# x1 read half a group earlier in a graph network kernel, its parts turned at the slot's head and normalised by VectorE

## The chip, the cores and the metric

One core of a Trainium2 chip. The metric is the device time of the program in microseconds (us), as the median of several executions. "Group", "part" and "half" below are the kernel's own units of work.

## The reference, cut to what matters

A graph of 12,500 nodes with 128 features each and 212,500 edges, sorted by destination, goes through two layers. The first is a relational layer (16 relation types, weights composed from 8 bases), the second takes the mean over the neighbours. Each is followed by a residual add and a layer norm without gain or bias.

```python
# layer 1: relational, W = sum over the bases
W = jnp.einsum('rb,bio->rio', w_comp, weight)
msg = jnp.einsum('ni,rio->rno', x, W)[etypes, src]
x1 = _layernorm(x + segment_sum(msg, dst) + h_bias)
# layer 2: mean of the neighbours
deg = jnp.maximum(segment_sum(ones, dst), 1.0)
agg = segment_sum(x1[src], dst)
out = _layernorm(x1 + x1 @ W_self + b_self + agg / deg[:, None] @ W_neigh)
```

## The kernel before

Edges are cut into chunks of 128 and groups of 8 chunks: 208 groups. GpSimd (POOL) gathers the source rows of a chunk with one indirect DMA, 128 rows at a time, into slots in SBUF, and TensorE (PE) sums them into short windows of destination nodes with a one-hot matrix as the moving operand. All order is written out by hand, as loops over g (the group) on each engine, with semaphores between them.

The two layers overlap. Since the edges are sorted by destination, x1 (the first layer's result) is finished front to back, in parts of 256 nodes (PART); part k is complete when all groups below done_at(k) = (17(k + 1) + 7) // 4 have been added, about every 4.25 groups, with 49 parts in all. The first PLAIN = 20 groups gather rows of x only (512 bytes, L1642, "narrow"). From group 20 on POOL gathers "wide" rows (1 KB, L1646) from a table in DRAM with x in the left half and x1 in the right half, where the part has been laid, and zeros where it has not. The table exists twice: in the upper copy the right half stays zero. Before the first wide group VectorE (DVE) marks the edges (mark_early): each half group h of 4 chunks reads x1 from the first front(h) parts, and an edge with a source beyond them goes to the upper copy. So half of the second layer's sum is made while the first layer still runs. The edges that were sent to the upper copy ("late" edges) are packed into full columns of 128 later on, and are gathered again in a second sweep (L1657 for two groups that were held back, L1673 for the rest) with x1 rows. How many columns are needed is fixed when the program is built, from front(h) and an even spread of sources; a flag checks the real data against it.

front(h) comes from READABLE, a distance in half groups: readable(h) = 4 (max(h - READABLE, 2) // 2 - 1) and front(h) = min(FRONT, readable(h) // 17), with FRONT = 44. With READABLE = 4 part k is read from half 2 done_at(k) + 4 on, the first half of group done_at(k) + 2. POOL waits, ahead of the first gather of each half, on the semaphores laid1 of the parts that are new in it (loop over `part`, in the GpSimd block), and on nothing else of theirs. Its slots hold four wide groups, so that for group g it also waits until the slot's last user has been read: `rows_read` for group g - 4, or, for g = 20 and 21, the sums (`z_done`) of the narrow groups 17 and 19.

How a part comes to be, at slot g = done_at(k):

- PE sums group g - 1 (sum_half, L2253, and for the x1 half early_half, L2265), ACT copies the sums out (L1722), PE multiplies them by the 8 bases (project, L2293), DVE adds them to acc (add_sums, L1904).
- PE transposes the part (turn_part, L2221), in program order behind sum_half(g, 0), the first half group's eight matmuls of g itself.
- DVE adds the transposed part to x (L1766), takes statistics (L1772, L1777), ScalarE (ACT) the root (L1690), DVE the reciprocal (L1784) and the shift (L1786), and ACT normalises in two activations, one for each tile of 128 nodes (normalise_quad, L1696).
- SyncE (SP) stores it into the table (L1533, laid1) and into x1_rows (L1535), and the degrees after them (L1526).

The order on DVE at slot g is: add_sums of a finished run, part_done, the pair additions (L1891), the one-hots of group g + 2 (scale, L1859 and L1865). PE's order is sum_half(g, 0), turn_part, early_half(g, 0), sum_half(g, 1), early_half(g, 1), project. Every fourth group PE also makes the coefficients of the next four groups (scale_by_relation, L2240).

Of the kernel before, what the change touches and what calls it, by code (L numbers as in the profile page):

```python
# [40 lines left out]
PART = TPP * P  # L41
PLAIN = 20
READABLE = 4
RUN = 5
# [13 lines left out]
def gnn_kernel(nc, x_in, src, dst, etype, weight, w_comp, h_bias, w_neigh, w_self, b_self, x1_rows, out):  # L58
# [48 lines left out]
    def front(h):  # L107
        return 0 if h < 2 * PLAIN else min(FRONT, readable(h) // 17)

    assert per_group % 2 == 0 and all((readable(h) * 3856) >> 16 == readable(h) // 17 for h in range(2 * groups))  # L110
    assert all(2 * done_at(front(h) - 1) + READABLE <= h < 2 * done_at(front(h)) + READABLE
               for h in range(2 * PLAIN, 2 * groups) if front(h) < FRONT)
    early_share = 16.0 / 17.0 / n_nodes

# [62 lines left out]
    with ctx:  # L177
# [340 lines left out]
        with nc.Block(no_gpsimd_drain=True) as block:  # L518
# [75 lines left out]
            def _(dve):  # L594
# [75 lines left out]
                dve.wait_ge(s_dl, 13)  # L670
                dve.wait_ge(s_held, 9)
                nc.vector.tensor_tensor(thr[:, 0:etiles], thr[:, 0:etiles], lates8[:, :], ALU.add).then_inc(s_held, 1)
                dve.wait_ge(s_held, 10)
                nc.vector.tensor_scalar(expected[:, :], thr[:, 0:etiles], -early_share * P, P * 16.0 / 17.0, ALU.mult,
# [38 lines left out]
                nc.vector.tensor_tensor(loop_n[:, :], loop_n[:, :], not_held[:, :], ALU.mult).then_inc(s_held, 1)  # L713
                dve.wait_ge(s_held, 11)
                nc.vector.tensor_tensor(lates[:, :], lates[:, :], loop_n[:, :], ALU.subtract).then_inc(s_order, 1)
# [486 lines left out]
        with nc.If(in_order):  # L1202
# [260 lines left out]
            with nc.Block(no_gpsimd_drain=True) as block:  # L1463
# [215 lines left out]
                def _(act):  # L1679
# [33 lines left out]
                    for g in range(groups + 8):  # L1713
                        if g * table_step < full_rows:
                            lay_zeros(g * table_step, min((g + 1) * table_step, full_rows))
                        if g in out_at:
                            roots_of(n1, out_at[g])
                            normalise_quad(n1, out_at[g])
                        if g < groups:
                            act.wait_ge(w1.z_done, g + 1)  # L1720
                            after(act, w1.y_done, run_of[g])
                            nc.scalar.copy(zsb[:, kept_at(g)].rearrange("p (h w) b n -> p h (w b n)", h=2),  # L1722
                                           zduos[g % 2]).then_inc(w1.z_copied, 1)
                        if g in loops_at:
                            q, m = quads[loops_at[g]]
                            act.wait_ge(s_loops, loops_at[g] + 1)
                            nc.scalar.copy(loops_b[:, q * P:(q + m) * P], tps[1][:, 0:m, :]).then_inc(s_loopc, 1)
                        if g in cleared_at:
                            clear_part(cleared_at[g])
# [29 lines left out]
                def _(dve):  # L1759
# [20 lines left out]
                    def quad_factors(n, k):  # L1780
# [6 lines left out]
                                                       op0=ALU.mult, op1=ALU.mult).then_inc(n.factors, 1)  # L1787

                    def part_done(k):
                        if k >= 2:  # L1790
# [5 lines left out]
                        quad_stats(n1, k)  # L1796
                        quad_factors(n1, k)

# [414 lines left out]
                def _(pe):  # L2213
# [85 lines left out]
                    for g in range(groups):  # L2299
                        coefficients_due = g % HALF == 2 and g // HALF + 1 < 2 * bodies  # L2300
                        if coefficients_due and g not in out_at:
                            scale_by_relation(g // HALF + 1)
                        sum_half(g, 0)
                        if g in out_at:
                            turn_part(out_at[g])
                            if coefficients_due:
                                scale_by_relation(g // HALF + 1)
                        early_half(g, 0)
                        sum_half(g, 1)
# [389 lines left out]
```

## Time and profile before

| | us |
|---|---|
| median of 3 executions | 3188.19 (3185.18 to 3188.43) |
| the profiled execution, its own time | 3178.99 |
| its span, first to last instruction | 3177.5 |
| PE busy | 2260.3 (71%) |
| DVE busy | 1554.4 (49%) |
| ACT busy | 316.0 (10%) |
| POOL busy | 2381.3 (75%) |
| mean granted TensorE clock | 0.681 of full speed |

The first layer's sweep, with the early half of the second, takes the span up to about 2102 us, the second sweep the rest. Busy time tells little here, as no engine is near 100%. What to read are the chain that ended last, the idle time of POOL with what ended it, and the order in time around one part. "Issue" is time in which an engine waited for nothing that the profile shows. The granted clock goes back and forth between full (2.4 GHz) and half (1.2 GHz) in stretches of 7 to 34 us, and the length of a matmul shows which of the two holds.

### The profile page before, as it was taken

To read this page: it belongs to the slowest core of one execution; us is meant where nothing else is said; L and a number is where in the kernel's file an instruction comes from. 1 tells how busy PE (TensorE), PEld (TensorE's weight loads), DVE (VectorE), ACT (ScalarE), POOL (GpSimd) and SP (SyncE) were. 2 spreads that over 40 slices of the span, in tenths; PEclk is the share of its full clock that TensorE was granted. 3 is DMA by queue.
4 is the path that set the end of the run, shared out by engine and by line. 5 is a ranking of instruction groups with operands and counts; after the bars stand their busy time and mean duration, and the time that the engine had idled before them with its cause. 6 is when DMAs were issued, how large, how long until landed. Compare 5 with 4: busy or idle time off the path is not lost.

```text
span 3177.5 us, 39386 instructions
## 1 busy us (share of the span) xinstructions
PE 2260.3 (71%) x13106; PEld 2164.2 (68%) x13106; DVE 1554.4 (49%) x4520; ACT 316.0 (10%) x619; POOL 2381.3 (75%) x2518
## 2 busy tenths in 40 slices
PE   2678888888878888898888888874555555555454
PEld 1568878888878888898887887864444444454444
DVE  6463333433343333333333333336677776877445
ACT  2111111111111111111111111100000000000012
POOL 7767777777777777777777777777777777777775
PEclk8887776776777777767777667665556555556567
DMA  4944444444444444444444444332222222222333
GB/s 115 312 132 122 121 122 118 121 123 121 123 120 121 119 122 122 122 122 123 122 115 123 123 122 120 111 97 53 63 63 63 73 63 63 73 63 73 89 82 87
DMA packets 257255, 345.05 MB, mean 109 GB/s; under 512 B 46912, under 2 KB 189861, under 8 KB 257046
## 3 DMA queue, kind: packets, MB, share of 16 engines
q0 software_dynamic: 104208, 262.76, 29.8%
q1 hardware_dynamic: 127398, 66.86, 7.1%
q10 hardware_dynamic: 25440, 12.85, 1.4%
q8 instruction: 106, 1.74, 0.2%
q14 instruction: 103, 0.84, 0.1%
HBM read 310.75 MB, written 44.38 MB: 112 GB/s over the span
## 4 chain that ended last, share of the span: by engine, by line
POOL 67%; issue 23%; PE 4%; DVE 1%; DMA 1%; ACTq 1%; ACT 1%; DVEq 0%; SPq 0%; POOLq 0%
POOL rows L1646 42%; POOL rows L1673 25%; PE zps L2253 1%; PE tps L2293 1%; ACTq L1683 1%; DMA rows<-x_x_rows,src_t 1%; POOL rows L1657 0%; DMA x_x_rows<-xout 0%; DVE acc L1904 0%; PE yps L2265 0%; ACT acc L1722 0%; PE tps L2240 0%; DMA erep<-in_edge_type_dram 0%; ACT xout L1696 0%; DVE xout L1766 0%
## 5 line engine op out<-in xcount | busy, mean ns | idle before, releaser
L1646 POOL DMA_INDIRECT rows<-x_x_rows,src_t x1501 | 1424.2, 949 | 469.5 <-issue 453.6
L2253 PE MATMUL zps<-acc,rows 128*128 128x168 f32 x3322 | 758.7, 388 | 285.2 <-DMA rows<-x_x_rows,src_t 280.5
L2253 PEld LDWEIGHTS zps<-acc,rows 128*128 128x128 f32 x3322 | 651.3, 246 | 307.6 <-DMA rows<-x_x_rows,src_t 197.0
L1673 POOL DMA_INDIRECT rows<-x_rows,picked_mem x685 | 647.9, 946 | 208.8 <-issue 208.8
L1904 DVE TENSOR_TENSOR acc<-acc,tps 128x21 f32 x831 | 146.7, 177 | 934.6 <-PE tps L2293 813.9
L2378 PE MATMUL zps<-acc,rows 128*128 128x128 f32 x1370 | 312.4, 400 | 403.2 <-DMA rows<-x_rows,picked_mem 389.4
L2378 PEld LDWEIGHTS zps<-acc,rows 128*128 128x128 f32 x1370 | 269.2, 292 | 438.2 <-DMA rows<-x_rows,picked_mem 270.5
L2293 PE MATMUL tps<-acc,picked_mem 128*128 128x168 f32 (+2 forms) x2288 | 488.5, 388 | 31.6 <-ACT acc L1722 22.6
L2265 PEld LDWEIGHTS yps<-oh,rows 128*128 128x128 f32 x3002 | 508.4, 248 | 0.0
L2293 PEld LDWEIGHTS tps<-acc,picked_mem 128*128 128x128 f32 x2288 | 454.0, 272 | 43.9 <-ACT acc L1722 24.7
L2265 PE MATMUL yps<-oh,rows 128*128 128x21 f32 x3002 | 478.5, 300 | 0.0
L1865 DVE TENSOR_TENSOR acc<-oh,tps 128x1344 f32<-128x1344 f32 x208 | 323.2, 1554 | 30.0 <-PE tps L2240 1.8
L1722 ACT COPY acc<-zps 128x672 f32<-128x672 f32 x208 | 149.0, 716 | 1410.2 <-PE zps L2253 1391.8
L1891 DVE TENSOR_TENSOR acc<-acc,yps 128x42 f32 (+1 forms) x831 | 163.3, 196 | 178.3 <-DVE acc L1891 45.2
L2104 DVE TENSOR_TENSOR acc<-place_b,tps 128x1024 bf16<-128x1024 bf16 x190 | 229.9, 1210 | 0.0
L2018 DVE TENSOR_TENSOR acc<-acc,zps 128x128 f32 (+1 forms) x442 | 118.1, 267 | 218.8 <-PE zps L2378 136.5
L1673 POOL DMA_INDIRECT rows<-x_rows,src_t x144 | 136.0, 944 | 43.9 <-issue 43.9
L2371 PE MATMUL zps<-oh,rows 128*128 128x21 f32 x320 | 74.6, 383 | 84.4 <-DMA rows<-x_rows,src_t 83.3
L1642 POOL DMA_INDIRECT rows<-in_x_dram,src_t x112 | 107.7, 961 | 34.2 <-issue 34.2
L2371 PEld LDWEIGHTS zps<-oh,rows 128*128 128x128 f32 x320 | 71.0, 328 | 88.5 <-DMA rows<-x_rows,src_t 52.1
L1993 DVE TENSOR_TENSOR acc<-picked_mem,tps 128x1024 f32<-128x1024 f32 (+2 forms) x92 | 104.8, 1140 | 0.0
L1690 ACT ACTIVATE std<-mv,epst 128x2 f32<-128x2 f32 (+1 forms) x74 | 21.9, 296 | 698.3 <-DVE mv L1777 698.3
(294 smaller groups left out, 1493.6 us busy)
## 6 DMA issues: line engine op xcount, KB each, us to landing
rows<-x_x_rows,src_t POOLq DMA_INDIRECT x1501, 2.8
erep<-in_edge_type_dram SPq DMA_DIRECT2D x207, 64.0 KB
x_x_rows<-zrow ACTq DMA_DIRECT2D x20, 576.0 KB, 3.7
x_x_rows<-in_x_dram SPq DMA_DIRECT2D x20, 576.0 KB
rows<-x_rows,picked_mem POOLq DMA_INDIRECT x685, 2.5
x_rows<-xout SPq DMA_DIRECT2D x49, 128.0 KB
xin<-in_x_dram SPq DMA_DIRECT2D x48, 128.0 KB
out_dram<-xout SPq DMA_DIRECT2D x24, 256.0 KB, 2.5
```

The lines of the kernel that those rows point to most:

```text
L1646: gather = pool.indirect_dma_start(out=wide_rows[:, g % WIDE_SLOTS, c, :], out_offset=None, in_=table, in_offset=bass.IndirectOffsetOnAxis ...
L1673: pool.indirect_dma_start(out=rows[:, j % SLOTS, c, :], out_offset=None, in_=x1_rows[0:n_nodes, :], in_offset=bass.IndirectOffsetOnAxis(ap ...
L1722: nc.scalar.copy(zsb[:, kept_at(g)].rearrange("p (h w) b n -> p h (w b n)", h=2), zduos[g % 2]).then_inc(w1.z_copied, 1)
L1865: nc.vector.tensor_tensor(a[:, g % 4], oh1[:, g % 6].unsqueeze(2).to_broadcast([P, CPG, n_bases, SPAN]), wcp[:, m % 2, g % HALF, :].rearra ...
L1891: add = nc.vector.tensor_tensor(target, target, windows_of(g)[:, first:2, c, :], ALU.add)
L1904: add = nc.vector.tensor_tensor(target, target, bank_of(run_of[g])[:, y0:y0 + SPAN], ALU.add)
L2104: nc.vector.tensor_tensor(to_lane[:, t % UNROLL], place_b[:, 0, at].unsqueeze(2).to_broadcast([P, CPG, P]), lanes_p.unsqueeze(1).to_broadc ...
L2253: last = nc.tensor.matmul(zwins[g % 2][:, c // HALF, c % HALF // 2], slot_rows(g, c), a[:, g % 4, c], start=(c % 2 == 0), stop=(c % 2 == 1 ...
L2265: last = nc.tensor.matmul(windows_of(g)[:, 0, c // 2], wide_rows[:, g % WIDE_SLOTS, c, d:2 * d], oh1[:, g % 6, c], start=(c % 2 == 0), sto ...
L2293: last = nc.tensor.matmul(bank_of(r)[:, y0:y0 + duos * SPAN].rearrange("p (w n) -> p w n", n=SPAN), wb[:, b, :], kept[:, 0:duos, b, :], st ...
L2371: last = nc.tensor.matmul(sums_of(j, c // 2, SPAN), rows[:, j % SLOTS, c, :], oh1[:, j % 4, c], start=(c % 2 == 0), stop=(c % 2 == 1))
L2378: last = nc.tensor.matmul(sums_of(j, c0, P), rows[:, j % SLOTS, c, :], oh2[:, j % 4, c, :], start=(c == c0), stop=(c == c0 + n - 1))
```

## The change

- READABLE goes from 4 to 3. Since readable(h) is rounded down to whole groups, this changes odd halves alone: part k is read from half 2 done_at(k) + 3 on, the second half of group done_at(k) + 1.
- The first four wide groups (SETTLING = 8 halves) read the first three parts alone (FIRST_PARTS); the threshold in `thr` gets the same bound by two more DVE instructions in the preamble.
- PE turns a part ahead of sum_half(g, 0).
- The part's normalisation moves from ACT to DVE: the shift and ACT's two activations go, and DVE does (x - mean) * rstd in place with two tensor_scalar instructions.

```diff
-READABLE = 4
+READABLE = 3
+FIRST_PARTS = 3
+SETTLING = 8
...
     def front(h):
-        return 0 if h < 2 * PLAIN else min(FRONT, readable(h) // 17)
+        if h < 2 * PLAIN:
+            return 0
+        return min(FIRST_PARTS if h < 2 * PLAIN + SETTLING else FRONT, readable(h) // 17)
...
-                dve.wait_ge(s_held, 9)
+                nc.vector.tensor_scalar(half_v[:, :], half_i[:, :], float(2 * PLAIN + SETTLING), FAR, ALU.is_ge,
+                                        ALU.mult).then_inc(s_held, 1)
+                dve.wait_ge(s_held, 10)
+                nc.vector.scalar_tensor_tensor(out=thr[:, :], in0=half_v[:, :], scalar=float(FIRST_PARTS * PART), in1=thr[:, :],
+                                               op0=ALU.add, op1=ALU.min).then_inc(s_held, 1)
+                dve.wait_ge(s_held, 11)
...
                         if g in out_at:
                             roots_of(n1, out_at[g])
-                            normalise_quad(n1, out_at[g])
...
+                    def normalise_part(k):
+                        dve.wait_ge(n1.std, k + 1)
+                        m = part_tiles(k)
+                        nc.vector.reciprocal(rstd[:, 0:m], std[:, 0:m]).then_inc(n1.rstd, 1)
+                        dve.wait_ge(n1.rstd, k + 1)
+                        for j in range(m):
+                            normed = x_out_of(n1, k)[:, j, :]
+                            last = nc.vector.tensor_scalar(normed, normed, mv[:, j, 0:1], rstd[:, j:j + 1], ALU.subtract, ALU.mult)
+                        last.then_inc(n1.norm, 1)
...
                         quad_stats(n1, k)
-                        quad_factors(n1, k)
+                        normalise_part(k)
...
-                        sum_half(g, 0)
                         if g in out_at:
                             turn_part(out_at[g])
                             if coefficients_due:
                                 scale_by_relation(g // HALF + 1)
+                        sum_half(g, 0)
                         early_half(g, 0)
```

## Rows read from the trace of the kernel before

**Rows 1.** The page, the chain that ended last: share of the span by engine.
```profile
POOL 67%; issue 23%; PE 4%; DVE 1%; DMA 1%; ACTq 1%; ACT 1%; DVEq 0%; SPq 0%; POOLq 0%
```
**Rows 2.** Groups by form: line, count | busy us, mean ns of one | idle before, releasers.
```profile
L1646 POOL DMA_INDIRECT rows<-x_x_rows,src_t x1501 | 1424.2, 949 | 469.5 <-issue 453.6 <-DMA x_x_rows<-xout 15.9
...
L1673 POOL DMA_INDIRECT rows<-x_rows,picked_mem x685 | 647.9, 946 | 208.8 <-issue 208.8
```
**Rows 3.** Waits of POOL: line, waited for, us in total, times, longest.
```profile
POOL rows L1646 <- DMA x_x_rows<-xout: 15.9, 12, 12.6
```
**Rows 4.** Timeline around the first wide group: start, us, engine, line, count, [idle before].
```profile
206.74 4.14 PE L2253 MATMUL zps<-acc,rows 128*128 128x168 f32 x16
...
216.16 3.64 PE L2253 MATMUL zps<-acc,rows 128*128 128x168 f32 x24
...
218.76 0.37 SPq L1533 DMA_DIRECT2D x_x_rows<-xout  x1
...
221.38 0.94 POOL L1646 DMA_INDIRECT rows<-x_x_rows,src_t  x1 [12.57 <-DMA x_x_rows<-xout]
```
**Rows 5.** Timeline, PE at group 20; part 4's store; the gather half a group ahead.
```profile
228.03 2.58 PE L2253 MATMUL zps<-acc,rows 128*128 128x168 f32 x8 [4.79 <-DMA rows<-x_x_rows,src_t]
...
264.23 0.36 SPq L1533 DMA_DIRECT2D x_x_rows<-xout  x1
...
266.35 0.95 POOL L1646 DMA_INDIRECT rows<-x_x_rows,src_t  x1 [0.30 <-DMA x_x_rows<-xout]
```
**Rows 6.** Timeline, part 31 at slot g = 137, all engines.
```profile
1403.61 2.52 PE L2253 MATMUL zps<-acc,rows 128*128 128x168 f32 x8
1403.96 1.14 DVE L1904 TENSOR_TENSOR acc<-acc,tps 128x21 f32 x4 [6.58 <-PE tps L2293]
...
1405.92 0.63 PE L2221 MATMUL tps<-ident,acc 128*128 128x128 f32 x2
...
1408.48 0.17 DVE L1784 RECIPROCAL rstd<-std 128x2 f32<-128x2 f32 x1 [0.43 <-ACT std L1690]
...
1408.87 0.88 ACT L1696 ACTIVATE xout<-xout,shift,rstd 128x128 f32<-128x128 f32 x2 [0.50 <-DVE shift L1786]
...
1409.67 0.95 POOL L1646 DMA_INDIRECT rows<-x_x_rows,src_t  x1 [0.30 <-issue]
1409.82 0.36 SPq L1533 DMA_DIRECT2D x_x_rows<-xout  x1
```
**Rows 7.** Timeline, part 26 at slot g = 116: its store, and the gather in question.
```profile
1195.66 0.36 SPq L1533 DMA_DIRECT2D x_x_rows<-xout  x1
...
1199.23 0.95 POOL L1646 DMA_INDIRECT rows<-x_x_rows,src_t  x1 [0.30 <-issue]
```
**Rows 8.** One group by form; then a gather and the VectorE instruction it met.
```profile
L2035 DVE TENSOR_SCALAR steps<-late_b 128x128 f32<-128x128 bf16 x11 | 2.9, 261 | 0.0
...
404.32 1.07 POOL L1646 DMA_INDIRECT rows<-x_x_rows,src_t  x1 [0.30 <-issue]
404.79 0.49 DVE L1852 TENSOR_SCALAR acc<-erep,rel_of_p 128x512 f32<-128x512 int32 x1
```
**Rows 9.** Timeline, part 6 (g = 31), then part 43 (g = 188).
```profile
341.99 0.18 DVE L1904 TENSOR_TENSOR acc<-acc,tps 128x21 f32 x1
...
342.98 0.52 PE L2221 MATMUL tps<-ident,acc 128*128 128x128 f32 x2
...
346.68 0.95 POOL L1646 DMA_INDIRECT rows<-x_x_rows,src_t  x1 [0.30 <-issue]
346.77 0.36 SPq L1533 DMA_DIRECT2D x_x_rows<-xout  x1
...
1920.58 0.36 SPq L1533 DMA_DIRECT2D x_x_rows<-xout  x1
1920.92 0.95 POOL L1646 DMA_INDIRECT rows<-x_x_rows,src_t  x1 [0.30 <-issue]
```
**Rows 10.** Timeline, VectorE in the preamble.
```profile
10.98 1.89 DVE L677 TENSOR_REDUCE stats<-acc 128x13 f32<-128x1664 int32 x1 [1.42 <-DMA acc<-in_src_dram]
```

More of the change, by code:

```diff
@@ L107, in front @@
     def front(h):
-        return 0 if h < 2 * PLAIN else min(FRONT, readable(h) // 17)
+        if h < 2 * PLAIN:
+            return 0
+        return min(FIRST_PARTS if h < 2 * PLAIN + SETTLING else FRONT, readable(h) // 17)
     assert per_group % 2 == 0 and all((readable(h) * 3856) >> 16 == readable(h) // 17 for h in range(2 * groups))
-    assert all(2 * done_at(front(h) - 1) + READABLE <= h < 2 * done_at(front(h)) + READABLE
-               for h in range(2 * PLAIN, 2 * groups) if front(h) < FRONT)
+    assert all(2 * done_at(front(h) - 1) + READABLE <= h for h in range(2 * PLAIN, 2 * groups))
+    assert all(h < 2 * done_at(front(h)) + READABLE
+               for h in range(2 * PLAIN + SETTLING, 2 * groups) if front(h) < FRONT)
     early_share = 16.0 / 17.0 / n_nodes
@@ L670, in _ @@
                 dve.wait_ge(s_dl, 13)
-                dve.wait_ge(s_held, 9)
+                nc.vector.tensor_scalar(half_v[:, :], half_i[:, :], float(2 * PLAIN + SETTLING), FAR, ALU.is_ge,
[4 more added lines that the diff above has]
+                dve.wait_ge(s_held, 11)
                 nc.vector.tensor_tensor(thr[:, 0:etiles], thr[:, 0:etiles], lates8[:, :], ALU.add).then_inc(s_held, 1)
-                dve.wait_ge(s_held, 10)
+                dve.wait_ge(s_held, 12)
                 nc.vector.tensor_scalar(expected[:, :], thr[:, 0:etiles], -early_share * P, P * 16.0 / 17.0, ALU.mult,
@@ L713, in _ @@
                 nc.vector.tensor_tensor(loop_n[:, :], loop_n[:, :], not_held[:, :], ALU.mult).then_inc(s_held, 1)
-                dve.wait_ge(s_held, 11)
+                dve.wait_ge(s_held, 13)
                 nc.vector.tensor_tensor(lates[:, :], lates[:, :], loop_n[:, :], ALU.subtract).then_inc(s_order, 1)
```

## The prediction

> **What bounds the kernel now.** I read the chain that ended last first: two thirds of the span lie on GpSimd (POOL) and 23% are "issue", the pause between two gathers [rows 1]. Then the gathers themselves: one of L1646 takes 949 ns and is followed by 453.6 us / 1501 = 302 ns of issue [rows 2], so POOL starts a gather every 1.25 us, and the second layer's go at the same pace [rows 2]. Last, what POOL waits for besides: landings of x1 in the table, 15.9 us in all [rows 3], and of these 12.57 us are one stall at the first wide group, g = 20 [rows 4]. The rest are the ordinary 0.30 us of issue, put down to a landing. So the time is the number of gathers times 1.25 us, plus one stall, plus a fixed head and tail. TensorE (PE), VectorE (DVE) and ScalarE (ACT) decide only through what they make POOL wait for. That is where to look: anything that makes POOL wait for a landed x1 part costs in full, since POOL never catches up.
>
> **The first stall.** At g = 20 the old rule asks for parts 0 to 3. Part 3's store is issued at 218.76 and the gather starts at 221.38, 2.62 us later [rows 4]: this is my price from a store's issue to the gather that waited for it, landing and wake-up together. The change asks for parts 0 to 2 only, and part 2 landed long before. But the next releasers stand close behind. Slot 0 wants the sums of group 17, done at 206.74 + 4.14 = 210.88, and slot 1 (g = 21) those of group 19, done at 216.16 + 3.64 = 219.80 [rows 4]. Both lie in a stretch in which PE and DVE take turns and POOL is two groups ahead, and the change makes them later: in groups 6, 10, 14 and 18 the turn stands ahead of the first half's eight matmuls, so these follow the wait instead of filling it. Following DVE's order through the timeline I get about 2 us more at group 17 and 3.4 us at group 19. With 0.5 us of waking POOL starts g = 20 at about 213.3 and g = 21 at 223.7, against 221.38 + 8 x 1.25 = 231.4: 7.7 us ahead. Most of it is then asked back by part 4. PE starts group 20 at 226.4 instead of 228.03, where it had waited 4.79 us for rows [rows 5]; it saves some 3 us up to part 4's turn and 0.6 us in the normalisation, so the store goes out near 260.6 instead of 264.23 and lets POOL go at 263.2. The new rule wants part 4 one half group earlier, at the gather that now starts at 266.35 [rows 5]. So 266.35 - 263.2 = about 3.2 us remain of the stall. Bounds: 0 (PE no earlier) and 7.7 (part 4 in time).
>
> **Gathers saved.** The planner's own formulas, worked out for both sets of constants: late edges 87,219 before and 86,903 after, late columns 846 and 844, gathers of the second layer 845 and 843, 111 late groups both times. Each part is readable half a group earlier (44 parts x 512 edges x 16/17 x 256/12500 = 434 edges fewer), and the four wide groups that leave out part 3 give back 79. Two gathers x 1.25 us = 2.5 us less. There is little to win here.
>
> **READABLE 4 to 3: what POOL then waits for.** The first gather that wants part k moves from the first half of group done_at(k) + 2 to the second half of the group before, 5.0 us earlier. The part comes no sooner than its chain allows: rows of the last group it needs, sums, projection, DVE's add, turn, add, statistics, root, normalise, store. Take part 31 (g = 137), where PE is at its low clock, 1.2 GHz: eight matmuls take 2.52 us [rows 6], against 3.64 us for 24 of them at 2.4 GHz [rows 4]. The last add ends at 1403.96 + 1.14 = 1405.10, but the turn starts at 1405.92, behind the half group's matmuls in PE's queue [rows 6]. At the slot's head it would start at about 1405.16: 0.76 us won. From the reciprocal's start at 1408.48 to the end of ACT's two activations (1408.87 + 0.88 = 1409.75) are 1.27 us [rows 6]. After the change DVE goes on by itself: 0.20 us for the reciprocal and 0.45 us for two subtract-and-multiply instructions (128x128 tensor_scalar: 261 ns each [rows 8], overlapped a little; 0.37 to 0.52 for both). 0.62 us won. The store moves from 1409.82 to 1408.44, and the gather that waits for it can start at 1408.44 + 2.62 = 1411.06. POOL would be there at 1409.67 [rows 6]. It waits 1.39 us.
>
> At the high clock the chain is short enough: part 26's store goes out at 1195.66, at least 0.62 us earlier after the change, so 1195.66 - 0.62 + 2.62 = 1197.66, and POOL comes at 1199.23 [rows 7]. No wait. I stepped through parts 4 to 43 in this way, each with its own turn, store and gather. Nineteen of the 40 come out with a wait, the first part 6 (last add's end 342.17, turn 342.98, so 0.75 us won there; store 346.77, gather 346.68: 1.34 us), the last part 43 (0.78 us won at the turn; store 1920.58, gather 1920.92: 0.88 us) [rows 9]; eleven are between 1.0 and 1.43 us, and the sum is 19.0 us. Without the two shortenings it would be 54 us in 30 parts; they are worth having, but about 1.4 us a part is not the 5.0 us that are asked for. POOL doesn't make a wait up, and it isn't undone by a neighbour: in nearly all of these parts the chain starts from rows that have just landed, so it moves along with POOL. With the chain 0.25 us shorter or longer the sum is 14 or 25 us; with the low clock in fewer or more of the parts I let it go from 5 to 30.
>
> **Who stands behind the new waits.** On PE the half group's matmuls now wait behind the turn for DVE's add. At part 31 that moves them from 1403.61 to about 1405.7; z_done, ACT's copy and the next projection go along, 2 us, while the slot's reuse by POOL is four groups (40 us) away. Free, unless PE fell behind for good; it waits for rows again before the next part. On DVE the two instructions replace a 0.16 us one: +0.3 us for the one-hots and pair additions queued behind. ACT loses 0.88 us of work a part, free. SP's queue keeps its order; its store is only released earlier. The two new 429-wide instructions of the preamble (a 1664-wide one takes 1.89 us, so some 1.0 us for both) fall into DVE's 1.42 us wait for a load [rows 10]: nothing.
>
> **DVE against POOL.** A gather met by DVE's 128x512 tensor_scalar took 1.07 us instead of 0.95 [rows 8]. 98 new instructions, each less than half as long, at 0.02 to 0.05 us: 2 to 5 us; I take 2. The Trainium skill speaks against this part of the change (page "SBUF — State Buffer", section "SBUF: two separate sides"): a DVE instruction in a two-port mode holds the port pair it shares with GpSimd, and a gather's descriptors can't be written until it ends. By that rule in full, 98 x 0.22 us = some 21 us in place of 2 (an estimate from the page's rule); the row shows only 0.12 us lost under an instruction of 0.5 us, so I stay with the row.
>
> **Sum**, against the profiled execution: -3.2 (first stall) - 2.5 (gathers) + 19.0 (parts) + 2 (DVE against POOL) = +15.3 us. The profiled execution took 3178.99 us, the median of the timed ones is 3188.19; the difference carries over, so 3188.19 + 15.3 = 3203.5 us, 0.48% slower.
>
> **Rivals.** (a) Faster: the waits for parts do not come, because PE is mostly at the high clock at the turns or the wake-up after a landing is cheaper in mid-stream than at g = 20, where several waits stand in a row. Then -7.7 - 2.5 + 2, and up to 2 us of scattered waits: 3181. It decides where the chain is 1.4 us shorter than I have it. For it: about half of the parts have no wait even by my sum. Against it: the start of the chain and the gather's time are read, not guessed. 0.12. (b) Balance: half the waits (9.5), the stall's whole 7.7 back: +1.3, 3189.5. 0.20. (c) The first stall stays, because group 17's and 19's sums, now later, hold POOL in place of part 3: part of that change then doesn't do what it is written for; +18.5, 3206.7. 0.15, slower as the forecast. (d) The port lock in full on top of the sum: +34, 3222. 0.05. The forecast itself: 0.48.
>
> **How the numbers follow.** About 0.2% (6.4 us) is what a measurement can tell from no change. Slower by more: forecast, (c), (d), 0.68. Within: (b), 0.20. Faster: (a), 0.12. The range leaves out (a) and (d) and takes in (b) and the bounds of the terms (waits from 5 to 30, stall from 0 to 7.7): 3184 to 3218.
>
> **What would show it.** The one 12.57 us stall should be gone and in its place a short wait of 4 to 5 us at g = 20 (on PE's sums) and one of some 4 us at the second half of g = 24. POOL's idle before L1646 put down to landings should have some twenty entries of 1 to 1.4 us, at the second halves of the groups done_at(k) + 1, and only where the half group's matmuls took about 2.5 us; the turn should start within 0.1 us of DVE's last add, and the store about 2.5 us after DVE's first add to xout. The gathers of L1673 should be 827. If POOL's idle on landings sums to under 5 us, or the store comes more than 2 us earlier after the rows than now, the term of 19 us is wrong; if gathers of over 1.0 us are more frequent by hundreds, it is the port.

## The result, and the profile after

The change makes the kernel slower. The median of the timed executions is 3210.66 us (3197.64 to 3213.19, four of them), beside 3187.48 us for the kernel before, measured with it: a ratio of 1.0067, 95% interval 1.0050 to 1.0085. The profiled execution took 3197.64 us with a span of 3196.1 us, against 3178.99 and 3177.5 before, so 18.65 us more; the mean granted clock is 0.671 (0.681 before). Forecast were 3203.5 us, slower, in a range of 3184 to 3218. The direction and the range hold, the time is 7 us off. The sum of the prediction was +15.3 us; the medians are 23.2 us apart.

| | before | after |
|---|---|---|
| median, us | 3187.48 | 3210.66 |
| profiled execution, us | 3178.99 | 3197.64 |
| POOL's waits at the first two wide groups, us | 12.3 | 8.8 |
| POOL's waits for later parts, us | 0 | 16.0 |
| gathers of the second sweep | 829 | 827 |

Here and below a wait is the idle time ahead of a gather less the 0.30 us that every gather has, and only those over 0.05 us count.

The page after, first the busy time of each engine:

```profile
PE 2284.0 (71%) x13102; PEld 2183.0 (68%) x13102; DVE 1579.2 (49%) x4570; ACT 275.6 (9%) x521; POOL 2386.4 (75%) x2516
```

ACT has lost 40 us and DVE gained 25: the normalisation has moved. That says nothing of the time. Next the groups of the page (line, engine, operation, count | busy us, mean ns | idle us before), with two lines for the second sweep:

```profile
L1656 POOL DMA_INDIRECT rows<-x_x_rows,src_t x1501 | 1429.6, 952 | 482.4 <-issue 451.2
...
L1683 POOL DMA_INDIRECT rows<-x_rows,picked_mem x683 | 647.5, 948 | 208.3 <-issue 208.3
...
L1683 POOL DMA_INDIRECT rows<-x_rows,src_t x144 | 136.4, 947 | 43.9 <-issue 43.9
```

Against [rows 2] the first sweep has 12.9 us more idle time and 5.4 us more busy time, and the second sweep two gathers fewer (683 for 685). What POOL waited for (line, waited for, us, times, longest):

```profile
POOL rows L1656 <- DMA x_x_rows<-xout: 21.8, 19, 2.2
...
POOL rows L1656 <- PE zps L2272: 9.4, 2, 5.6
```

In place of the one long stall of [rows 3] stand 19 landings of x1, 16 of them with a wait in them, none over 1.9 us, and two waits for sums that were not there before. The first two wide groups in the timeline (start, us, engine, line, [idle before]), to be laid beside [rows 4]:

```profile
211.60 2.48 PE L2272 MATMUL zps<-acc,rows 128*128 128x168 f32 x16
...
214.36 0.94 POOL L1656 DMA_INDIRECT rows<-x_x_rows,src_t  x1 [5.63 <-PE zps L2272]
...
218.53 1.14 DVE L1923 TENSOR_TENSOR acc<-acc,tps 128x21 f32 x4 [0.22 <-PE tps L2312]
...
219.72 0.69 PE L2240 MATMUL tps<-ident,acc 128*128 128x128 f32 x2 [1.20 <-DVE acc L1923]
...
220.20 1.81 PE L2259 MATMUL tps<-wc_blk,acc 128*128 128x64 f32 x8
...
221.80 5.84 PE L2272 MATMUL zps<-acc,rows 128*128 128x168 f32 x32
...
223.15 0.36 SPq L1543 DMA_DIRECT2D x_x_rows<-xout  x1
...
227.92 0.95 POOL L1656 DMA_INDIRECT rows<-x_x_rows,src_t  x1 [3.78 <-PE zps L2272]
```

Part 3's store, which POOL waited for before, now goes out at 223.15, when POOL has long begun. What holds POOL at 214.36 are the sums of group 17, done at 214.1, and at 227.92 those of group 19: the 32 matmuls of groups 18 and 19 now all stand behind the turn and are done at 227.64, where they had been done at 219.80 [rows 4].

One part in full, part 33 (g = 146), the longest wait of all:

```profile
1505.25 1.14 DVE L1923 TENSOR_TENSOR acc<-acc,tps 128x21 f32 x4 [6.99 <-PE tps L2312]
...
1506.44 0.69 PE L2240 MATMUL tps<-ident,acc 128*128 128x128 f32 x2 [1.20 <-DVE acc L1923]
...
1507.33 0.42 DVE L1775 TENSOR_TENSOR xout<-xin,tps 128x256 f32<-128x256 f32 x1 [0.95 <-PE tps L2240]
...
1508.99 0.17 DVE L1801 RECIPROCAL rstd<-std 128x2 f32<-128x2 f32 x1 [0.36 <-ACT std L1700]
...
1509.19 0.60 DVE L1805 TENSOR_SCALAR xout<-xout,mv,rstd 128x128 f32<-128x128 f32 x2
...
1509.87 0.36 SPq L1543 DMA_DIRECT2D x_x_rows<-xout  x1
...
1512.84 0.94 POOL L1656 DMA_INDIRECT rows<-x_x_rows,src_t  x1 [2.15 <-DMA x_x_rows<-xout]
```

The turn follows the last add by 0.05 us, DVE goes straight from the reciprocal to the two normalising instructions, and the store follows them. From the first add to xout to the store it is 2.54 us. Both shortenings work, and POOL still waits 1.85 us.

### The profile page after: what moved, and what is told of

It reads as the page before. It is cut to its first block and busy times, and to the rows that moved or that the text cites. A ratio compares the mean times of both kernels' runs of the same rounds, so it can differ in the third digit from the quotient of the medians.

```text
span 3196.1 us, 39239 instructions
## 1 busy us (share of the span) xinstructions
PE 2284.0 (71%) x13102; PEld 2183.0 (68%) x13102; DVE 1579.2 (49%) x4570; ACT 275.6 (9%) x521; POOL 2386.4 (75%) x2516
## 5 line engine op out<-in xcount | busy, mean ns | idle before, releaser
L2272 PE MATMUL zps<-acc,rows 128*128 128x168 f32 x3322 | 766.5, 391 | 228.3 <-DMA rows<-x_x_rows,src_t 224.1
L2272 PEld LDWEIGHTS zps<-acc,rows 128*128 128x128 f32 x3322 | 660.6, 249 | 247.4 <-DMA rows<-x_x_rows,src_t 191.4
L2397 PE MATMUL zps<-acc,rows 128*128 128x128 f32 x1366 | 319.9, 408 | 395.9 <-DMA rows<-x_rows,picked_mem 388.7
L2397 PEld LDWEIGHTS zps<-acc,rows 128*128 128x128 f32 x1366 | 276.0, 300 | 431.5 <-DMA rows<-x_rows,picked_mem 263.9
L2284 PEld LDWEIGHTS yps<-oh,rows 128*128 128x128 f32 x3002 | 520.5, 253 | 0.0
L2312 PE MATMUL tps<-acc,picked_mem 128*128 128x168 f32 (+2 forms) x2288 | 476.0, 380 | 33.8 <-ACT acc L1731 24.6
L2284 PE MATMUL yps<-oh,rows 128*128 128x21 f32 x3002 | 485.6, 303 | 0.0
L2312 PEld LDWEIGHTS tps<-acc,picked_mem 128*128 128x128 f32 x2288 | 440.6, 265 | 46.9 <-ACT acc L1731 29.6
L2127 DVE TENSOR_TENSOR acc<-acc,tps 128x320 bf16<-128x320 bf16 (+2 forms) x190 | 90.0, 474 | 0.0
```

Source lines behind the costliest of these rows:

```text
L2272: last = nc.tensor.matmul(zwins[g % 2][:, c // HALF, c % HALF // 2], slot_rows(g, c), a[:, g % 4, c], start=(c % 2 == 0), stop=(c % 2 == 1 ...
L2284: last = nc.tensor.matmul(windows_of(g)[:, 0, c // 2], wide_rows[:, g % WIDE_SLOTS, c, d:2 * d], oh1[:, g % 6, c], start=(c % 2 == 0), sto ...
L2312: last = nc.tensor.matmul(bank_of(r)[:, y0:y0 + duos * SPAN].rearrange("p (w n) -> p w n", n=SPAN), wb[:, b, :], kept[:, 0:duos, b, :], st ...
L2397: last = nc.tensor.matmul(sums_of(j, c0, P), rows[:, j % SLOTS, c, :], oh2[:, j % 4, c, :], start=(c == c0), stop=(c == c0 + n - 1))
```

## The experiments

They ran in three series, each on another chip and with executions of the kernel before of its own (medians 3179.97, 3180.32 and 3179.67 us). The first has the four kernels from the base line to FIRST_PARTS alone, the second the next four, the third the last three. Ratios are within a series; two kernels of different series are compared by their ratios. Line numbers differ from kernel to kernel. POOL's waits are given in two sums, at the first two wide groups and for the parts behind them; they and the span are of one profiled execution, the median is of four or ten executions. The profile lines are of POOL's waits, in the columns as above, unless told otherwise.

**The base line.** The kernel before, unchanged.

> The kernel before, unchanged, for its spread and for the pace of the gathers. In the changed kernel's profiled execution a gather takes 947 ns in the median against 945 before, in the first 160 gathers and in the second sweep too, where nothing was changed; over 2504 gathers that is some 6 of the 17.6 us by which the last gather starts later. Theory A (the pace belongs to the execution or the chip, not to the kernel): this run's profile differs from the first profile of before in the median too, by 1 to 4 ns either way. Theory B (VectorE's new instructions slow the gathers): 945 again, and a span within 2 us of 3177.5.

Measured: 3180.32 us, ratio 1.0001 (0.9991 to 1.0010), span 3179.6 us, gathers at the old pace (median 946 ns, 945 in the first profile of this kernel). That alone decides between neither theory; the kernel after, again, does. One wait at the first wide group, 13.3 us, none for parts.

```profile
POOL rows L1646 <- DMA x_x_rows<-xout: 16.9, 12, 13.6
```

**READABLE 3 alone.** The rest is the kernel before.

```diff
-READABLE = 4
+READABLE = 3
```

> READABLE 3 alone: turn behind the half group's matmuls, ScalarE normalises, part 3 still asked for at g = 20. By the waits for parts: 30 of the 40 parts wait, 54 us by the prediction's stepping with 2.62 us from store to gather; the changed kernel shows about 2.3 us for it, so 45 us. The 12.57 us stall stays, three gathers fewer give 3.75 us: 41 to 50 us slower, 3229 to 3238. Rival (PE lags less once POOL waits, so that waits don't add up): under 25 us.

Measured: 3229.33 us, ratio 1.0155 (1.0138 to 1.0172), span 3225.6 us, 826 gathers in the second sweep.

```profile
POOL rows L1646 <- DMA x_x_rows<-xout: 72.1, 32, 9.7
```

9.4 us of this are the stall at g = 20, and 52.9 us lie in 29 waits for parts. The prediction had worked out 54 us in 30 parts for this case; by the shorter time from store to gather that the kernel after shows, the expectation above made it 45. READABLE alone is by far the dearest part of the change, and saves three gathers.

**Everything but READABLE.** The kernel after, with READABLE = 4.

```diff
-READABLE = 3
+READABLE = 4
```

> The changed kernel with READABLE 4. By the waits: POOL waits for no part, the two waits at g = 20 and 21 on PE's sums stay at 5.3 + 3.5 = 8.8 us in place of 12.3, one gather more than before costs 1.25: 2 us faster than before, 3185. Rival (turning at the head or normalising on VectorE costs by itself, through PE falling behind or through the port): 5 to 20 us slower than before with waits of POOL elsewhere or longer gathers.

Measured: 3179.69 us, ratio 0.9995 (0.9985 to 1.0005), span 3180.1 us. No waits for parts, 9.8 us at the first two wide groups. I had expected 2 us less time than before; the two can't be told apart.

```profile
POOL rows L1656 <- PE zps L2272: 10.4, 2, 6.6
POOL rows L1656 <- DMA x_x_rows<-xout: 5.5, 18, 0.3
```

The whole loss of the change goes with READABLE: with READABLE 4 no part is waited for, and the time is that of before. It also shows that the first stall has not become cheap: sums of groups 17 and 19 hold POOL nearly as long as part 3 did.

**FIRST_PARTS alone.** The kernel before with the rule for the first four wide groups, and nothing else (with it the two instructions for `thr` in the preamble, as in the change).

```diff
-        return 0 if h < 2 * PLAIN else min(FRONT, readable(h) // 17)
+        if h < 2 * PLAIN:
+            return 0
+        return min(FIRST_PARTS if h < 2 * PLAIN + SETTLING else FRONT, readable(h) // 17)
...
```

> Before with FIRST_PARTS and SETTLING alone (READABLE 4, turn and normalisation as before). The narrow groups' chain isn't made later: group 17's sums end at 210.9, so g = 20 starts at about 211.4 after a wait of some 2.3 us, g = 21 doesn't wait, and part 4, wanted at the first half of g = 25, comes 1 to 3 us late. Stalls 12.3 before, 4 to 5 after, one gather more: 6 to 7 us faster, 3181. Rival (the early waits are handed on in full to part 4, as the prediction had it): 0 to 3 us faster.

Measured: 3171.09 us, ratio 0.9971 (0.9961 to 0.9980), span 3175.3 us. One wait of 5.8 us at g = 20, on the sums of group 17; none at g = 21; one gather more. This part of the change gains 9 us of time where it stands alone, more than the 6 to 7 expected: no part came late.

```profile
POOL rows L1656 <- PE zps L2273: 6.1, 1, 6.1
```

**The kernel after, again.**

> The changed kernel once more, on the same footing as the others: waits for parts 14 to 21 us, 8.8 us at g = 20 and 21 in place of 12.3, two gathers fewer: 8 to 15 us slower than before. And if the slower pace of its first profile (947 ns a gather) belonged to that execution or chip, this profile has 945 or 946 again; if it is the kernel's, 947.

Measured: 3200.50 us, ratio 1.0061 (1.0045 to 1.0078), span 3198.6 us; 11.6 us at the first two wide groups and 21.5 us in 19 parts. That is 20 us slower than before, where I had expected 8 to 15: both sums of waits are larger than in the first profile (8.8 and 16.0). Gathers are back at a median of 946 ns.

```profile
POOL rows L1656 <- DMA x_x_rows<-xout: 27.9, 21, 2.5
POOL rows L1656 <- PE zps L2272: 12.2, 2, 6.8
```

**The turn back behind the half group's matmuls.** READABLE 3, FIRST_PARTS and DVE's normalisation stay.

```diff
+                        sum_half(g, 0)
                         if g in out_at:
...
-                        sum_half(g, 0)
                         early_half(g, 0)
```

> The changed kernel with the turn behind the half group's matmuls again. Stepping through the parts of before with 2.3 to 2.6 us from store to gather and 0.54 us won in the normalisation gives 30 to 38 us of waits in 26 to 28 parts; the waits at g = 20 and 21 shrink to the 5.8 us of the run with FIRST_PARTS alone. 21 to 29 us slower than before, and 8 to 14 slower than the changed kernel. Rival (the moved turn costs PE as much as it gives the part): within 4 us of the changed kernel.

Measured: 3202.38 us, ratio 1.0075 (1.0057 to 1.0093), span 3199.4 us. I had expected it clearly slower than the kernel after; it is level with it. The waits say why:

```profile
POOL rows L1656 <- DMA x_x_rows<-xout: 43.2, 28, 2.7
```

The parts do cost more, 34.6 us in 28 waits against 21.5 in 19, so the turn at the head is worth 13 us there, as far as one profile of each tells. But the two waits at the start of the wide groups are gone altogether. The narrow groups run faster in this order, here the run-up to group 20:

```profile
204.05 2.48 PE L2272 MATMUL zps<-acc,rows 128*128 128x168 f32 x16
...
210.20 1.34 PE L2272 MATMUL zps<-acc,rows 128*128 128x168 f32 x8
...
211.85 0.44 PE L2240 MATMUL tps<-ident,acc 128*128 128x128 f32 x2 [0.30 <-DVE acc L1923]
...
212.97 3.64 PE L2272 MATMUL zps<-acc,rows 128*128 128x168 f32 x24
```

Eight matmuls fill the time in which PE would wait for DVE's add (0.30 us of it is left), and group 19 is done at 216.61, 11 us ahead of the kernel after. Not all of this is the order around this turn: group 17 is already done at 206.53 in place of 214.08.

**ScalarE normalises, as before.** The rest is the kernel after.

```diff
                             roots_of(n1, out_at[g])
+                            normalise_quad(n1, out_at[g])
...
                         quad_stats(n1, k)
-                        normalise_part(k)
+                        quad_factors(n1, k)
```

> The changed kernel with ScalarE's normalisation again. By the same stepping 26 to 35 us of waits in 26 to 29 parts, 9 us at g = 20 and 21: 20 to 29 us slower than before, 8 to 14 slower than the changed kernel. Rival (VectorE's two instructions hold up the gathers by the port or their own queue): within 4 us of the changed kernel, or faster.

Measured: 3212.28 us, ratio 1.0100 (1.0083 to 1.0117), span 3206.8 us; 7.7 us at the first wide groups, 36.0 us in 24 parts.

```profile
POOL rows L1656 <- DMA x_x_rows<-xout: 44.0, 26, 2.6
```

I had expected 20 to 29 us slower than before, and it is 32. Without the shorter normalisation the parts cost 14.5 us more than in the kernel after again: POOL waits in half of the parts, so that some half a microsecond more in each counts that often, and in five parts more. Only about half of it is the chain itself, which is 14.18 us on the mean here and 13.92 there; from a store to the gather that waited for it are 2.69 us, there 2.46. What makes this second time longer was not settled.

**Less work on PE.** The kernel after, with every second matmul of early_half left out: half of the second layer's early sums are then missing. They stay whole where a turn follows.

```diff
-                            for c in half_of(g, h):
+                            whole = g + 1 in out_at and h == 1
+                            for c in half_of(g, h) if whole else half_of(g, h)[::2]:
...
-                                                        start=(c % 2 == 0), stop=(c % 2 == 1 or c == real_chunks(g) - 1))
+                                                        start=(c % 2 == 0),
+                                                        stop=(not whole or c % 2 == 1 or c == real_chunks(g) - 1))
```

> The changed kernel with every second matmul of early_half left out, except in the half group right ahead of a part's slot, so that a part's own chain keeps its length and PE has about 100 us less to do: this leaves half of the early x1 sums out of the computation. If the low clock at the turn decides which parts wait, the clock is low at fewer turns, and the waits for parts fall in that proportion (16 us to under 8 us), those at g = 20 and 21 stay: 8 us or more faster than the changed kernel. Rival (the chain is short by the same amount whatever the clock, because rows and adds set it): waits for parts stay within 3 us of the changed kernel's.

Measured: 3211.56 us, ratio 1.0092 (1.0075 to 1.0109), span 3211.9 us; 35.2 us in 27 parts. I had expected fewer waits, and there are more. The stretch from 250 to 2100 us, this kernel and then the kernel after again (busy us of each engine, granted clock, DMA share, GB/s):

```profile
250.00:2100.00 1850.00, 1395.40 (x7105) 1351.93 (x7104) 719.93 (x2297) 168.36 (x308) 1374.12 (x1447) 0.70 0.42 118
```

```profile
250.00:2100.00 1850.00, 1588.20 (x8458) 1555.71 (x8457) 726.03 (x2322) 169.71 (x311) 1384.35 (x1458) 0.70 0.42 119
```

PE had 193 us less to do (about 100 expected) and the granted clock stayed at 0.70, so the chip did not give back a higher clock for it. At the parts it was worse: the sums ahead of the turn ran at 1.2 GHz in 25 of 40 parts (14 in the kernel after again) and the turn in 33 of 40 (29). The chain lengthened by 0.49 us, from 13.92 to 14.41 us on the mean, measured from the last gather that a part needs to its store, and the waits followed. More turns at the low clock went with more waits, as the first of the two expectations has it, but the kernel did not lower their number, which it was made for: that the clock sets which parts wait rests on finding the two together and not on a test, and what sets the clock is not shown.

**The turn at the head in the wide groups only.** The narrow groups get the old order.

```diff
+                        if narrow(g):
+                            sum_half(g, 0)
                         if g in out_at:
...
-                        sum_half(g, 0)
+                        if not narrow(g):
+                            sum_half(g, 0)
```

> The changed kernel, but in the narrow groups (below 20) the turn stands behind the half group's matmuls again. If the moved turn costs only there, by group 19's sums coming later (5.3 + 3.5 and 6.5 + 5.2 us at g = 20 and 21 in the changed kernel's two profiles, 0 in the run with the turn put back everywhere), the waits at g = 20 and 21 fall to 0 to 6 us and those for parts stay at 16 to 21: 5 to 12 us faster than the changed kernel, 8 to 15 slower than before. Rival (the early start is handed on to parts 4 and 5): within 3 us of the changed kernel, with new waits at g = 24 and 28.

Measured: 3194.04 us, ratio 1.0060 (1.0039 to 1.0080), span 3188.4 us; 3.0 us at the first wide groups, 19.6 us in 22 parts.

```profile
POOL rows L1656 <- PE zps L2272: 3.3, 1, 3.3
...
POOL rows L1656 <- DMA x_x_rows<-xout: 27.0, 24, 2.6
```

By POOL's waits it has both advantages, the short start and the shorter chain: 22.6 us in all, against 33.1 in the kernel after again, and no wait at parts 4 to 6 that hands the early start back. By time the gain is not clear: its median is 6.5 us lower, but on another chip, and the two ratios to before, 1.0060 and 1.0061, don't differ; the profiled execution is the fastest of its four (3189.77 to 3204.54).

**The best of the parts.** READABLE 4, FIRST_PARTS, DVE normalises, the turn in its old place.

```diff
-READABLE = 3
+READABLE = 4
...
+                        sum_half(g, 0)
                         if g in out_at:
...
-                        sum_half(g, 0)
                         early_half(g, 0)
```

> READABLE 4, the bound on the first four wide groups, VectorE's normalisation, turn behind the half group's matmuls: every piece that made POOL wait taken out. By the waits: none for parts, 0 to 6 us at g = 20, one gather more than before: 5 to 11 us faster than before, level with or up to 5 us faster than FIRST_PARTS alone. Rival (VectorE's two instructions cost by themselves): 3 or more us slower than FIRST_PARTS alone.

Measured: 3170.70 us, ratio 0.9972 (0.9962 to 0.9982), span 3169.0 us. It is faster than before and after both, but no faster than FIRST_PARTS alone (3171.09 us, ratio 0.9971).

```profile
POOL rows L1656 <- PE zps L2272: 1.4, 2, 1.1
POOL rows L1656 <- DMA x_x_rows<-xout: 4.6, 15, 0.3
```

Of the 13.3 us stall 0.8 are left. The profiled execution of FIRST_PARTS alone had 5.8 us left and took 3176.67 us, the slowest of its ten (3167.83 to 3176.67), so the gap between the two spans (6.3 us) is mostly one of that execution, and DVE's normalisation earns nothing here either.

**DVE's normalisation alone.** The kernel before with it.

```diff
-                            normalise_quad(n1, out_at[g])
...
-                        quad_factors(n1, k)
+                        normalise_part(k)
```

> Before with the normalisation on VectorE alone, READABLE 4. The 12.3 us stall shrinks by the 0.5 us by which the store comes sooner, and nothing else waits: 0 to 1 us faster than before if the new instructions don't hurt the gathers, 1 to 4 us slower if they cost 0.02 to 0.05 us each as the prediction had it, 20 us slower by the port lock in full.

Measured: 3179.87 us, ratio 1.0002 (0.9993 to 1.0012), span 3179.8 us. With no waits for parts the shorter chain buys nothing, and the 98 instructions on DVE cost nothing that can be measured.

**The account of all runs.** POOL's waits and its gathers explain the span of every kernel in the three series. Take the 3179.6 us of the base line, add the waits less 13.3, and 1.25 us for each gather more or less:

| kernel | first waits | part waits | gathers | worked out | span |
|---|---|---|---|---|---|
| READABLE 3 alone | 9.4 | 52.9 | -3 | 3224.9 | 3225.6 |
| after, again | 11.6 | 21.5 | -2 | 3196.9 | 3198.6 |
| turn back | 0 | 34.6 | -2 | 3198.4 | 3199.4 |
| ScalarE normalises | 7.7 | 36.0 | -2 | 3207.5 | 3206.8 |
| less work on PE | 11.1 | 35.2 | -2 | 3210.1 | 3211.9 |
| head in wide groups | 3.0 | 19.6 | -2 | 3186.4 | 3188.4 |
| all but READABLE | 9.8 | 0 | +1 | 3177.4 | 3180.1 |
| FIRST_PARTS alone | 5.8 | 0 | +1 | 3173.4 | 3175.3 |
| best of the parts | 0.8 | 0 | +1 | 3168.4 | 3169.0 |
| DVE's normalisation | 13.0 | 0 | 0 | 3179.3 | 3179.8 |

No span is further than 2.7 us from its sum, while the spans reach from 3169 to 3226. The first profile of the kernel after is not in the table: its sum would be 3188.6 us and its span is 3196.1, for the reason given below.

## Why the prediction was right, and where it was off

**What bounds the kernel.** Right. A wait of POOL costs in full: the table above shows it in ten profiles.

**The waits for parts (19.0 us).** Right in mechanism, and near in size: 16.0 us in 16 parts in the first profile, 21.5 in 19 in the second, forecast 19.0 in 19. Eleven of the 16 are of 1.0 us or more, as forecast, though the longest is 1.85 and not 1.43. Without the two shortenings it was to be 54 us; READABLE 3 alone showed 52.9. Which parts wait was less exact: part 6 waited 1.10 us (forecast 1.34), part 43 0.13 (0.88), and part 31, the worked example, did not wait at all: the sums ahead of its turn ran almost wholly at the high clock (0.95 granted), and where the clock is low shifts from execution to execution. The link to the clock holds, as far as two things found together can show it: of the 40 parts 23 were turned at the low clock, and 14 of these have a wait; of the 17 at the high clock two have one. The eight matmuls of sums ahead of the turn separate them better: where they had a granted clock under 0.75, in 12 parts, all 12 wait; of the other 28 only four do. These eight take 2.61 us at the low clock and 1.41 at the high one.

The rule behind it can be read from the same trace. From the start of the last gather that a part needs to the first gather that wants it are 13 gathers at 1.25 us, 16.3 us; less 2.1 to 2.3 us from the store to the gather, the chain may take some 14 us. In the first profile it takes 14.22 to 15.23 us in each of the 16 parts that wait, and at most 14.08 us in each of the 24 that don't. With READABLE 4 there were 17 gathers, 21.3 us, for a chain of 14.85 us on the mean.

The steps within it: the turn now starts 0.06 us after the last add in all 40 parts, where it had been 0.70 us on the mean, so the whole gap is won. DVE's normalisation was mis-sized: I had 0.45 us for the two instructions, from a 261 ns row of another form [rows 8], and they take 0.60.

```profile
L1805 DVE TENSOR_SCALAR xout<-xout,mv,rstd x98: 339/346/556, 132.8 to 2134.0; 128x128 f32<-128x128 f32 x98
```

(This is one group: min/median/max in ns.) With f32 in and out and two factors read from SBUF, it is a third slower than that row's form, bf16 in and two constants; which of these differences costs the time was not tried. From the first add to xout to the store it is 2.56 us on the mean of 40 parts, before 3.08: 0.52 us won, not 0.62. Against this the price from a store to the waiting gather was too high: for the 13 waits over 0.7 us it is 2.25 to 2.98 us, median 2.34, and I had taken the 2.62 us of g = 20 for all. The two errors pull opposite ways, by 0.10 and 0.28 us. By the prediction's own slope (a chain 0.25 us shorter gives 14 us in place of 19), the 0.18 us that remain make 15 to 16 us, an estimate: near the 16.0 of the first profile, and short of the 21.5 of the second.

**The first stall (-3.2 us).** The number came out, -3.5 us in the first profile and -1.7 in the second, but by luck and for another reason than I gave. Two steps failed, the delay of group 19's sums and the wait for part 4. Group 17's sums came at 214.1, forecast 212.9. Group 19's came at 227.64 and not at 223.2: 7.8 us later than before, where I had 3.4. The larger piece lies ahead of the turn. DVE's last add before it had started at 213.85,

```profile
213.85 1.14 DVE L1904 TENSOR_TENSOR acc<-acc,tps 128x21 f32 x4 [2.06 <-PE tps L2293]
```

and now starts at 218.53, 4.7 us later, 3.2 of which came with group 17. The other 3.1 us lie behind the add. In the old order eight of the 32 matmuls of groups 18 and 19 run ahead of the turn, in PE's wait for DVE (1.34 us); now all 32 follow a wait of 1.20 us, a turn and eight coefficient matmuls at the low clock (0.69 and 1.81 us; 0.44 and 1.00 us before), and take 5.84 us where they had taken 4.98. I had counted the moved matmuls, but neither all of the delay that reaches the turn nor that the clock might be low there. So POOL waited another 3.5 us at g = 21. And the wait for part 4 at g = 24, which was to ask most of the gain back, did not come: the part was stored at 259.07, sooner than forecast, and POOL was at its gather only at 263.00, already late. Just there it was to be released by my sum (263.2), which is why the number came out. This is rival (c) in part: the sums held POOL in place of part 3. The turn at the head is not free in the narrow groups. All kernels with FIRST_PARTS show it: 7.7 to 11.6 us are waited at the first two wide groups in the five profiles with the turn at the head in the narrow groups, and 0 to 5.8 us in the four with the old order. So FIRST_PARTS can give back 7 to 13 us of a stall of some 13, and the order of the narrow groups takes most of that again. The four values with the old order (0, 0.8, 3.0 and 5.8 us) also show how far this start varies for another reason, which was not found.

**Gathers (-2.5 us).** Right, 827 in the second sweep. (The two pieces given for it, 434 edges fewer and 79 back, make 355 and not the 316 of the totals; the number of gathers comes from the totals.)

**DVE against POOL (+2 us).** Nothing that the time can tell: with 98 such instructions added to the kernel before, the ratio is 1.0002, interval 0.9993 to 1.0012, so 4 us more at most, and the span is 0.2 us longer. The term of 2 us is neither shown nor excluded by it. The traces show a little of it: in the first profile of the kernel after 71 wide gathers meet one of these instructions and take 983 ns on the mean, the rest 951, which makes 2.3 us, if the meeting is the cause; with DVE's normalisation alone 48 meet one, 961 against 950 ns, 0.6 us. Gathers of over 1.0 us are hardly more frequent (46 of the 1501 wide ones, 37 before), so the sign that I had named for the port did not show. The row that I took the price from was a dear one: 52 gathers meet that 128x512 instruction in the trace before, with a median of 946 ns and a mean of 988. By the Trainium skill's rule (page "SBUF — State Buffer", section "SBUF: two separate sides") it could have been some 21 us, the estimate of the prediction; that is five times what the interval leaves, so the measurement decides against the estimate, and rival (d) falls. Whether these instructions run in a two-port mode, which the rule asks for, no run shows.

**What wasn't in the sum.** In the first profile of the kernel after the gathers took longer throughout: the median of all 2504 is 947 ns, before 945. Here are the wide ones (min/median/max ns):

```profile
L1656 POOL DMA_INDIRECT rows<-x_x_rows,src_t x1501: 943/949/1465, 214.4 to 2119.8; - x188
```

POOL was busy for 5.1 us more (2386.4 against 2381.3) with two gathers fewer, which are 1.9 us: 7.0 us for the pace, the meetings with DVE above among them. Of the 18.65 us, 12.5 are waits (16.0 - 3.5), -2.5 the gathers, 7.0 this pace, and 1.7 are left over, 1.0 of them behind the start of the last gather. The same kernel in the second series had a median of 946 ns, as before:

```profile
L1656 POOL DMA_INDIRECT rows<-x_x_rows,src_t x1501: 940/946/1484, 214.8 to 2122.8; - x188
```

So the pace belongs to that execution or chip, not to the change. In the second series the forecast +15.3 us stands beside a span 19.0 us longer and a median 20.2 us longer than the kernel before again. In the first comparison the timed executions of after lie 13 us above its profiled one and those of before 9 us; why the two differ was not settled.

**The rivals.** (a) fell: the waits came. One of its two conditions was partly true, since the time from store to gather is 0.28 us shorter than at g = 20, but it asked for a chain 1.4 us shorter. (b) fell with it. (c) holds in its mechanism and not in its size: sums do hold POOL in place of part 3, and 1.7 to 3.5 us of the stall went all the same. (d) fell.

## What to carry to other kernels

Where one engine issues work at a fixed pace and never catches up, list its waits and add them: that sum and the number of gathers told the spans of ten profiles within 2.7 us, and the eleventh but for 7 us of slower gathers. Before a wait is moved earlier, write down the chain that it waits for and its slack at the slower clock; a request 5 us earlier against a chain 1.2 to 1.4 us shorter brought 16 to 21 us of waits where there had been none, to save 2.5 us of work. And a reordering that helps in one phase (the turn at the head, in the wide groups) can cost as much in another where the same engines take turns (by POOL's waits in the second series, 13 us gained for the parts and 12 lost at the start), so try it phase by phase.

## What was not expected of the hardware

- Less matmul work did not raise the granted clock (above). With the order of PE's work it did change: over the four executions of each, the kernel after again was granted 0.661 to 0.668 and the kernel with the turn back 0.684 to 0.689. Where the turn is at the head it fell on the low clock at 23 to 33 of the 40 parts, where it is behind at 7 to 19 (counted by a mean granted clock under 0.75 in the two matmuls). So the turn at the head shortens the chain and slows it at once. That the turn then comes directly behind a wait of PE for DVE may be the cause; this was not tried by itself.
- The indirect gathers were slower in a single execution from end to end (medians of 949 against 946 ns on the wide rows, 947 against 945 on all), which came to 7 us in this kernel.
- When group 17's sums are done differs from kernel to kernel (ACT's copy of them starts at 206.6 us with the turn back and at 216.4 with less work on PE), also between kernels with the same narrow groups (208.7 in the best of the parts, 211.6 with the head in the wide groups only). Why was not settled.
- The stretches in which one granted clock holds were given as 7 to 34 us at the start. In the trace before they are of 3 to 31 us between 250 and 2100 us, and in the second sweep up to 201 us.
